# Expert blocks numbered in three levels, with the first 16 tiles' rows sent ahead of the next 8

## What is computed

```python
x = layernorm(x + attention(x))            # 16 heads of width 8, biases, head mask
x = layernorm(x + moe(x))
# moe(x): xf is [4096, 128]
shared = gelu(xf @ Wfc_s + bfc_s) @ Wproj_s + bproj_s        # 128 -> 512 -> 128
probs  = softmax(xf @ Wr)                                    # 8 experts
topk_p, topk_i = top_k(probs, 2);  topk_p /= sum(topk_p)
routed = sum over the token's 2 experts e of gate_e * (gelu(xf @ Wfc[e] + bfc[e]) @ Wproj[e] + bproj[e])
out = shared + routed
```

## Time and profile before

| | us |
|---|---|
| median of 3 runs (lowest, highest) | 517.65 (517.15, 518.68) |
| profiled execution, device time | 515.57 |
| its span in the trace | 513.8 |

### The profile page before, as it was taken

How to read it: one execution, slowest core, us unless ns; L and a number is a source line. 1 busy time by engine, 2 the same in 40 slices (tenths; PEclk the granted TensorE clock), 3 DMA queues, 4 the chain that set the end, 5 groups by cost and what they waited for, 6 DMA issues and landing times. The chain is left out here.

```text
span 513.8 us, 13680 instructions
## 1 busy us (share of the span) xinstructions
PE 418.1 (81%) x4871; PEld 277.4 (54%) x4871; DVE 361.1 (70%) x765; ACT 329.2 (64%) x624; POOL 322.4 (63%) x427
## 2 busy tenths in 40 slices
PE   4999999999999999999965888604999999999000
PEld 2444454555545555545542665503999999998000
DVE  3567888787888788788681698502778777777582
ACT  1147888788878888878714997302666776676162
POOL 4402678566573758565356666666688778877651
PEclk9999999999999999999986999956999999999655
DMA  3322554635454455521101111145371111117142
GB/s 87 89 59 65 157 158 115 177 102 145 115 159 122 138 142 157 166 76 34 42 17 46 43 49 43 48 113 156 101 210 42 49 44 48 43 31 264 50 147 61
DMA packets 63110, 50.25 MB, mean 98 GB/s; under 512 B 7339, under 2 KB 54581, under 8 KB 63045
## 3 DMA queue, kind: packets, MB, share of 16 engines
q1 hardware_dynamic: 58500, 40.91, 28.0%
q0 software_dynamic: 4544, 8.47, 5.2%
HBM read 24.96 MB, written 22.95 MB: 93 GB/s over the span
## 5 line engine op out<-in xcount | busy, mean ns | idle before, releaser
L553 DVE TENSOR_REDUCE row_max<-s_ps 128x2 f32<-128x512 f32 x256 | 164.9, 683 | 45.7 <-PE s_ps L684 43.7
L413 ACT ACTIVATE probs<-ring_ps 128x1024 f32<-128x1024 f32 x128 | 130.7, 1022 | 46.3 <-PE ring_ps L702 45.9
L1496 POOL DMA_INDIRECT results<-gated,rows_in x78 | 91.9, 1178 | 26.5 <-issue 22.6
L1652 ACT ACTIVATE hid<-h_ps,bias 128x256 f32<-128x256 f32 x156 | 61.1, 474 | 64.3 <-PE h_ps L1586 64.3
L684 PE MATMUL s_ps<-qk_stack 24*128 24x256 f16 x512 | 83.5, 271 | 7.1 <-DVE row_max L553 2.6
L1337 POOL DMA_INDIRECT slots<-rows,slot_at x64 | 65.8, 1028 | 29.4 <-issue 17.2
L702 PE MATMUL ring_ps<-qk_stack 26*128 26x256 f16 x512 | 83.0, 271 | 0.0
L720 PE MATMUL av_ps<-probs,v_aug 128*32 128x256 f32 x1024 | 68.5, 385 | 0.0
L684 PEld LDWEIGHTS s_ps<-qk_stack 24*128 24x128 f16 x512 | 33.8, 92 | 61.5 <-issue 32.4
L1604 PE MATMUL y_ps<-w,hid 128*128 x312 | 57.7, 220 | 0.0
L1605 PE MATMUL y_ps<-w,hid 128*128 x312 | 57.5, 219 | 0.0
(11 more groups left out here) (218 smaller groups left out, 953.6 us busy)
## 6 DMA issues: line engine op xcount, KB each, us to landing
qk_stack<-qk_rows SPq DMA_DIRECT2D x64, 96.0 KB
slots<-empty_row SPq DMA_DIRECT2D x13, 390.0 KB, 5.0
qk_rows<-qk_parts SPq DMA_DIRECT2D x16, 256.0 KB, 2.6
rows<-results SPq DMA_DIRECT2D x8, 512.0 KB, 6.5
rows_in<-slots SPq DMA_DIRECT2D x2, 1300.0 KB, 9.5
w_stage<-in_w_fc SPq DMA_DIRECT2D x9, 256.0 KB, 3.2
w_stage<-in_w_proj SPq DMA_DIRECT2D x9, 256.0 KB, 3.7
rows_in<-slots SPq DMA_DIRECT2D x1, 2080.0 KB, 10.2
```

Source lines behind the costliest of these rows:

```text
L413: nc.scalar.activation(probs[:, n % PROBS], ring(key), ACT.Exp, scale=SCORE_SCALE).then_inc(ring_emptied, 1)
L553: nc.vector.tensor_reduce(row_max[:, h], s1_ps[:, h % 2], AX_X, ALU.max, negate=True).then_inc(max_done, 1)
L1496: nc.gpsimd.indirect_dma_start(out=a["results"][:, :], out_offset=bass.IndirectOffsetOnAxis(ap=rows_in[:, 2 * n + half, DEST:DEST + 1].bit ...
L1652: mm = nc.scalar.activation(hid[:, cols], h_ps[:, cols], ACT.Gelu_apprx_tanh, scale=1.0 / UNIT, bias=bias[:, n, c:c + 1])
```

## The change

The router is rewritten so that the blocks of the first 24 tiles are numbered in three levels: blocks that are full after 16 tiles, blocks that become full by tile 24, and the part-filled rest. The routing passes stay (`PASSES`, 24 and 8 tiles), but rows are sent in three shares (`SENT`): 32 sends for tiles 0 to 15 (first, then second choices), 16 for tiles 16 to 23, 16 for the last 8. SP loads `slots` in six pieces; the first two (tiles 0 to 2 and 2 to 18) need only the first 32 sends, the third (18 to 34) 48, the rest all 64. In step 17 both `pick`s now stand ahead of all else on DVE, the counts come behind pair 3 and not 5, `gate` and the first `place` move from step 18 to the end of step 17. In step 18 two sends stand ahead of `make_x1` and four at the end. The table is made in two parts.

```diff
-SHARES = ((0, 24), (24, 32))
+PASSES = ((0, 24), (24, 32))
+SENT = ((0, 16), (16, 24), (24, 32))
-PLACED = {18: (0, 4)}
+PLACED = {18: (2, 4)}
-Q_AT, K_AT, TURN_AT, LOGIT_AT, COUNT_AT = 0, 3, 2, 6, 5
+Q_AT, K_AT, TURN_AT, LOGIT_AT, COUNT_AT = 0, 3, 2, 6, 3
...
                 if t == ROUTE_STEP:
                     logits_taken(0)
                     router.pick(0, 0)
+                    router.pick(0, 1)
...
-                if t == ROUTE_STEP:
-                    router.pick(0, 1)
                 if t == ROUTE_STEP + 1:
-                    router.gate(0)
-                    router.place(0, 0)
+                    router.place(0, 1)
...
                 if t == ROUTE_STEP:
+                    router.gate(0)
                     counts_taken(0)
                     router.tally(0)
-                    router.fill_whole()
-                    router.begin_parts()
-                    router.claim(0)
-                    router.offset(0)
-                    router.rank(0)
+                    router.level()
+                    router.lay_out()
+                    router.order(0)
+                    router.jump_levels()
+                    router.place(0, 0)
                 if t == ROUTE_STEP + 1:
-                    router.place(0, 1)
-                    router.move_on(0)
+                    router.carry()
...
+    def level(self):
+        n = PASSES[0][1]
+        up_to, reached = a["up_to"][:, 0:n * EXPERTS].rearrange("p (e t) -> p e t", e=EXPERTS), a["reached"]
+        for k, (_, tiles) in enumerate(SENT[:-1]):
+            self.blocks_of(up_to[:, :, tiles - 1:tiles], ALU.is_ge, 1, MOST_FIRST, reached[:, k + 1])
+        self.blocks_of(up_to[:, :, n - 1:n], ALU.is_gt, 0, MOST_FIRST, reached[:, LEVELS])
+        then(nc.vector.tensor_scalar(reached[:, 1:LEVELS + 1], reached[:, 1:LEVELS + 1], float(BLOCK), None, ALU.mult))
+
+    def lay_out(self):
+        then(nc.vector.tensor_tensor(fills[:], reached[:, 1:LEVELS + 1], reached[:, 0:LEVELS], ALU.subtract))
+        then(nc.vector.tensor_tensor_scan(passing[:, 0:LEVELS].rearrange("p l e -> p (l e)"), a["ones"][:],
+                                          fills[:].rearrange("p l e -> p (l e)"), 0.0, ALU.mult, ALU.add))
+        then(nc.vector.tensor_tensor(begins[:], passing[:, 0:LEVELS], fills[:], ALU.subtract))
+        then(nc.vector.tensor_tensor(moved[:], begins[:], reached[:, 0:LEVELS], ALU.subtract))
+        then(nc.vector.tensor_tensor(jumps[:], moved[:, 1:LEVELS], moved[:, 0:LEVELS - 1], ALU.subtract))
...
+    def jump_levels(self):
+        for k in range(LEVELS - 1):
+            self.jump(0, self.a["passing"][:, k], self.a["jumps"][:, k])
...
             nc.gpsimd.indirect_dma_start(...)\
-              .then_inc(a["rows_placed"][int(c > 0)], 16)
+              .then_inc(a["rows_placed"][c], 16)
...
-        FIRST, FULL, LOAD = 2, 2 * FULL_BLOCKS, 20
+        LOADS = (0, 2, 2 * FULL_BLOCKS[0], 2 * FULL_BLOCKS[1], 44, 60, SLOT_TILES)
...
-            sp.wait_ge(a["rows_placed"][0], 16 * TOP * SHARES[0][1])
-            load_slots(0, FIRST, first_loaded)
-            load_slots(FIRST, FULL, full_loaded)
-            sp.wait_ge(a["rows_placed"][1], 16 * TOP * (TOKEN_TILES - SHARES[0][1]))
+            sp.wait_ge(a["rows_placed"][0], 16 * TOP * (SENT[0][1] - SENT[0][0]))
+            load_slots(0)
+            load_slots(1)
+            sp.wait_ge(a["rows_placed"][1], 16 * TOP * (SENT[1][1] - SENT[1][0]))
+            load_slots(2)
+            sp.wait_ge(a["rows_placed"][2], 16 * TOP * (SENT[2][1] - SENT[2][0]))
             sp.wait_ge(table_made, 1)
-            for lo in range(FULL, SLOT_TILES, LOAD):
-                load_slots(lo, min(lo + LOAD, SLOT_TILES), rest_loaded)
+            for k in range(3, len(LOADS) - 1):
+                load_slots(k)
```

More of the change, by code:

```diff
@@ L500, in step @@
                     evacuate("k", ahead, bk)
+                if t == ROUTE_STEP:
+                    share_gap(nc, act, a, 0)
+                    take_counts(0)
                 if late.exists():
@@ L896 @@
 GROUPS = TOKEN_TILES // GROUP
-EARLY_PLACED = 1
 EMPTY_TILES = 6
@@ L900 @@
 PAUSE_EVERY = 8
[L901 to L904, removed]
+FULL_BLOCKS = tuple(hi - (EXPERTS - 1) for lo, hi in SENT[:-1])
+EARLY_BLOCKS = PASSES[0][1] + EXPERTS - 1
+EARLY_GROUPS = PASSES[0][1] // GROUP
+LEVELS = len(SENT)
 BLOCK = 2 * P
@@ L954, in make_moe_buffers @@
     a["slot_at"] = sb("slot_at", [P, TOP, TOKEN_TILES], U32)
[L955 to L958, removed]
+    for name, rows in (("reached", LEVELS + 1), ("passing", LEVELS + 1), ("fills", LEVELS), ("begins", LEVELS), ("moved", LEVELS),
+                       ("jumps", LEVELS - 1)):
+        a[name] = sb(name, [P, rows, EXPERTS])
+    most = max(hi - lo for lo, hi in PASSES)
     a["rest"] = sb("rest", [P, most, EXPERTS])
@@ L968, in make_moe_buffers @@
     a["full"] = sb("full", [P, EXPERTS, MOST_BLOCKS])
-    a["filled"] = sb("filled", [P, EXPERTS])
-    for name in ("extra", "fresh", "delta", "base", "some", "more"):
+    for name in ("taken", "base", "more", "fresh", "starts", "last_jump"):
         a[name] = sb(name, [P, EXPERTS])
@@ L1024, in share_of @@
 def share_of(tile):
-    return [c for c, (lo, hi) in enumerate(SHARES) if lo <= tile < hi][0]
+    return [c for c, (lo, hi) in enumerate(SENT) if lo <= tile < hi][0]
 def make_routing_constants(nc, pool, a, b32):
-    ident_h, before, ones16, pick, not_first, counting, number, from_end, block_start, rows1, rows2 = (
+    ident_h, before, ones16, pick, not_first, counting, number, from_end, first_row, rows1, rows2 = (
         a[k] for k in ("ident_h", "before", "ones16", "pick", "not_first", "counting", "number", "from_end",
-                       "block_start", "rows1", "rows2"))
+                       "first_row", "rows1", "rows2"))
     routing_consts = a["routing_consts"]
@@ L1148, in split @@
         dve.wait_ge(a["routing_consts"], ROUTING_CONSTS)
-        then(nc.vector.memset(a["taken"][:, 0], 0.0))
+        then(nc.vector.memset(a["reached"][:, 0], 0.0))
     def find(self, c, k):
         nc, a, then = self.nc, self.a, self.then
-        tiles, n = slice(*SHARES[c]), SHARES[c][1] - SHARES[c][0]
+        tiles, n = slice(*PASSES[c]), PASSES[c][1] - PASSES[c][0]
         TE = [P, n, EXPERTS]
@@ L1197, in gate, with blocks_of @@
         then(nc.vector.tensor_copy(a["rows1"][:, tiles, GATE:GATE + 1], gate1.unsqueeze(2)))
+    def blocks_of(self, tokens, compare, first, most, to):
+        nc, a, then = self.nc, self.a, self.then
+        EM = [P, EXPERTS, most]
+        full = a["full"][:, :, 0:most]
+        then(nc.vector.tensor_tensor(full, tokens.to_broadcast(EM), a["first_row"][:, first:first + most].unsqueeze(1).to_broadcast(EM),
+                                     compare))
+        then(nc.vector.tensor_reduce(to, full, AX_X, ALU.add))
@@ new lines, in add_blocks @@
+    def add_blocks(self):
+        nc, a, then = self.nc, self.a, self.then
+        more, fresh, starts, passing = a["more"], a["fresh"], a["starts"], a["passing"]
+        then(nc.vector.tensor_tensor_scan(fresh[:], a["ones"][:, 0:EXPERTS], more[:], 0.0, ALU.mult, ALU.add))
+        then(nc.vector.tensor_tensor(passing[:, LEVELS], fresh[:], passing[:, LEVELS - 1, EXPERTS - 1:EXPERTS].to_broadcast([P, EXPERTS]),
+                                     ALU.add))
+        then(nc.vector.tensor_tensor(starts[:], passing[:, LEVELS], more[:], ALU.subtract))
+        then(nc.vector.tensor_tensor(a["last_jump"][:], starts[:], passing[:, LEVELS - 1], ALU.subtract))
@@ L1326, in send @@
             n = a["sent_so_far"] = a.get("sent_so_far", -1) + 1
[L1327 to L1328 removed]
+            c = [c for c, (lo, hi) in enumerate(SENT) if TOP * lo <= n < TOP * hi][0]
+            lo, hi = SENT[c]
             k, tile = (n - TOP * lo) // (hi - lo), lo + (n - TOP * lo) % (hi - lo)
             if tile == lo:
[L1331 to L1334 removed]
+                routed = [c for c, (first, end) in enumerate(PASSES) if first <= lo < end][0]
+                pool.wait_ge(a["slots_known"], TOP * routed + k + 1)
+                if n == 0:
+                    pool.wait_ge(a["slots_emptied"], 16 * -(-SLOT_TILES // EMPTY_TILES))
                 if k == 1:
```

215 lines of the change are left out of this document (88 added, 127 removed).

## The result

| | before | after |
|---|---|---|
| median (lowest, highest), us | 517.40 (516.23, 518.68) | 522.71 (522.57, 524.03) |
| ratio, 95% interval | | 1.0095 [1.0056, 1.0134] |
| profiled span, us | 513.8 | 521.1 |

The forecast was 517.2, no change; the time is 5.3 us over before and above the upper end of the range, 521.9. In three of the five later groups of runs the kernel before itself took 548 to 561 us, with waits of ACT and DVE that the profile puts down to no engine ("remote", which no profile of a 517 us group has); from those I read single rows only, and the times told for the edits are those of the groups in which it took 517.7 to 517.9.

The account below looks back on a forecast made before the run. POOL's full queue of sends was taken as the bound: its start +0.55, landings -1.0, holds and tail unchanged, so -0.45 on 517.65 gives 517.2 us, no change; the range for 8 in 10 was 511.9 to 521.9.

Parts of the forecast that it names:

- POOL is full and sets the end: POOL's queue of sends is full from step 18 (261.64) to 484.0 us, and the end hangs on it.
- Rival C: The end hangs on PE after all, so its start 19.5 us earlier counts: 498 us; chance 0.03.
- PE's start: PE goes from the shared expert to block 0 at about 333 us, without its wait of 22.5.
- the `gated` stall: PE stops 8 to 10 us for a `gated` buffer, whose first results land near 375 to 377.
- POOL's start: POOL waits for the first `slots_known` and starts at 262.2, not 261.64: +0.55 us, bounds 0 and +2.5.
- mostly ahead of the counts: In the router's chain on DVE, `gate`'s 4 instructions take 0.95 us, mostly before the counts arrive (from 252.7).
- 39 blocks, 39 holds, the sum doesn't change: POOL's sends are held about 0.4 us per block whenever blocks run, so total holds stay the same.
- the forecast 1.0: Three landings fall beside blocks, where a late POOL is held less: -1.0 us, bounds 0 and -2.6.
- The hold's cause: One send per block takes 1.39 us, held 0.41 by DVE's `halve`, put to its instruction of 1.22.
- Rivals A and B: A: holds partly go, 508.9 or 511.9, chance 0.22. B: two holds a block, a quarter gives 521.9, chance 0.20.
- The Trainium skill's exclusive lock: By the shared-port rule alone, `halve`'s whole 1.22 could hold a send: 3.8 a block, 32 us more over 39 blocks.
- Tail 29.8: From POOL's end at 484.0 to the span's end at 513.8 stays 29.8 us.

Follow-up runs that it names:

- changed, again: The changed kernel run once more, unedited, as reference beside later edits: 524.5 us, ratio to before 1.0133.
- pick put back: Changed kernel with the second `pick` again behind batch 13's residual and the later reductions of step 17: 518.4 us, ratio to before 1.0010.
- loads late: Changed kernel with SP's first two `slots` loads waiting for all sends of the first 24 tiles: 521.8 us, ratio to before 1.0067.
- both: Changed kernel with the second `pick` put back and the first two `slots` loads made late: 518.3 us, ratio to before 1.0021.
- before, pick ahead: Kernel before with only its second `pick` moved right behind the first: 523.2 us, ratio to before 1.0119.
- changed, low half out: Changed kernel with `halve`'s second instruction cut to 8 of 1024 columns in blocks: 517.9 us, ratio to before 1.0000.

## Why the prediction was wrong

All eight comparable profiles, cut at the same points (us; "sends" is the busy time of 64 + 78 sends, "landings" POOL's waits for them, "rest" what is left of the run):

| kernel | pick to run | run | sends | landings | rest | last part | median |
|---|---|---|---|---|---|---|---|
| before | 18.85 | 222.38 | 157.7 | 14.8 | 49.9 | 5.8 | 517.4 |
| changed | 21.82 | 224.32 | 160.8 | 13.8 | 49.7 | 7.2 | 522.7 |
| changed, again | 22.38 | 224.83 | 158.9 | 13.5 | 52.4 | 7.2 | 524.5 |
| pick put back | 18.56 | 223.63 | 156.7 | 17.1 | 49.8 | 7.2 | 518.4 |
| loads late | 22.19 | 221.71 | 155.6 | 16.3 | 49.8 | 7.2 | 521.8 |
| both | 18.55 | 222.55 | 156.8 | 16.0 | 49.8 | 7.1 | 518.3 |
| before, pick ahead | 22.98 | 222.00 | 158.1 | 14.0 | 49.9 | 5.9 | 523.2 |
| changed, low half out | 22.31 | 217.73 | 152.9 | 15.0 | 49.8 | 7.2 | 517.9 |

- **POOL is full and sets the end: right.** The run is sends plus landings plus 49.8 us, to 0.1, in every kernel (52.4 less the one wait of 2.75 is 49.7). Rival C, PE's start counts, is out: 11 us of it moved nothing.
- **PE's start and the `gated` stall: right.** No wait ahead of the first block, then 8.48 us at 383.96 against the 8 to 10 forecast near 370 to 380. The start, 339.72 and not 333, was late by 6.7; with the pick put back it is 334.3.
- **POOL's start, +0.55 with an upper bound of 2.5: the step that failed.** The prediction saw that PE waits for `z` behind the second pick and put "about 2.1 of that" on PE. The wait was 2.58. Missing was what a wait does to PE behind it: the granted clock fell, and ring products and turned heads took up to 1.8 times as long. In all, the pick ahead costs 3.0 to 4.1 us from first pick to POOL's run, and in one profile 2.75 more at the next `z`. The bound of 2.5 assumed that a wait costs its own length. The second part of the step that failed is `gate`, "mostly ahead of the counts": DVE, itself waiting for PE's slow matmuls, began it at 255.34 and ended it 1.2 *behind* the counts, 0.5 of it in the one instruction of 0.72. Behind the first pick the forecast has the counts at 10.2, the scan at 10.9 and POOL at 19.4; measured are 11.8, 13.05 and 21.8. The chain from the scan to `slots_known` took the forecast 8.4.
- **"39 blocks, 39 holds, the sum doesn't change": too simple.** The result sends kept their sum, 91.5 against 91.9, where the row sends rose by 3.5, to 69.3: 16 of them beside blocks were stretched by 5.4 in total, against 2.0 for 8 before. Result sends did run free during the `gated` stall, six in a row at 0.98, but behind it they paid again: of the seven from 386.36 to 396.04 six took 1.06 to 1.69. Landings gave back the forecast 1.0. So +1.9, not -1.0. In other profiles of early loading sends and landings sum to 172.4 and 173.8; the before kernel has 172.5. The term is 0 to +2.
- **The hold's cause: the right function, the wrong instruction.** The 0.41 beside `halve` was put to its instruction of 1.22. It comes from the one of 0.69 ahead of it, of which 0.53 is left when the send starts; the 1.22 holds sends that start during it, such as the one at 414.17, by 0.59. Rivals A and B didn't decide: L1488's mean is 1.172.
- **The Trainium skill's exclusive lock** (SBUF — State Buffer, "SBUF: two separate sides"), weighed in the prediction. The Trainium skill says there that whichever of the two starts first has the shared port pair for its whole instruction, and that the other fully blocks. This case's traces agree for the send: it ends 0.86 behind the end of the halving instruction that ran when it started, 440 times of 440. The prediction took the rule to mean the whole 1.22, but that instruction starts 0.57 into the send; of the one that runs when the send starts 0.53 is left, and the send grows from 0.98 to 1.39.
- **Tail 29.8: off by 1.4.** To the last normalisation it is the same, 23.94 and 23.95. The part behind it takes 7.1 to 7.2 in all six profiles with the changed source and 5.8 to 5.9 in both with the old. No row shows what it is made of.

As the sum of its own steps the prediction lacks 2.4 at POOL's start, 2.9 in the run, and 1.4 at the end; the remaining 1.0 is the first piece of the table above, which isn't the change's. Only POOL's start is shown by experiment, in both directions: -6.1 and +5.5 us in the times, more than the piece itself, since the slow clock can also make POOL wait later on. What the other two cost in the times is not shown. The ends of the range, 511.9 and 521.9, were counted from the 517.65 of before and not from the forecast of 517.2; the time lies outside either way.

None of the kernels told by their time is faster than the one before beyond its interval; the change with the pick put back is level with it.

## What to carry to other kernels

Ask of every moved instruction which PE instruction waits behind it, and price a new wait of PE at more than its length: the work behind it may run at the lower clock. Where a queue is full and stands between two engines, the earlier start of one of them was worth nothing here; what counts is when the full queue starts and what lengthens its entries. Before blaming one instruction for a hold, look which one is running when the held one starts, and find rows in which each suspect runs alone.

## What the runs showed of the hardware

- A wait of PE of 2.6 us was followed by the lower level of its clock, for about a third of 10 us in one execution (0.83) and for 20 us in another (0.52, 0.50), with PE busy 9.2 and 10.0 of each 10 us there. With the same work and no such wait the clock of 250 to 260 was 1.00 in three profiles of three.
- An indirect send left alone takes 0.96 to 0.98 us. One that starts while DVE runs a halving instruction on 128x1024 float32 in SBUF ends 0.86 behind that instruction's end (440 of 440 for the one-input instruction), so it is held by what is left of it less 0.12. A float16 copy out of PSUM holds nothing (12 of 12).
- 44 sends queued without a wait between them went with single waits of 24.6 us of ACT and 24.0 of DVE that no engine of the profile ended, in a group where the kernel before took 561 us; the cause isn't shown.
